# Feed-forward stage of a gated attention kernel: normalised x turned by HBM regrouping and VectorE instead of by TensorE

## What is computed

```
x = x + tanh(g_xattn) * attention(layernorm(x), ctx)      # 16 heads, 77 context rows
x = x + tanh(g_ffn)   * ffn(layernorm(x))

def ffn(x):
    hidden = x @ W1 + b1                                  # 512 -> 2048
    imag = w_imag * sin(theta + hidden * 0.1)
    phase = cos(theta) * w_real + sin(theta) * w_imag
    act = relu(hidden + phase * imag * 0.1)
    return act @ W2 + b2                                  # 2048 -> 512
```

## Time and profile before

| what | value |
|---|---|
| runs (three) | 2257.52, 2258.82, 2259.79 us |
| median | 2258.82 us |
| span of the profiled execution | 2257.7 us |
| TensorE busy | 2212.9 us, 98% |
| VectorE busy | 1412.5 us, 63% |
| ScalarE busy | 1210.5 us, 54% |
| GpSimd busy | 407.9 us, 18% |
| mean rate of the DMA | 61 GB/s |

### The profile page before, as it was taken

The page is one execution under the profiler, slowest core; times in us unless marked ns, Lnnn a source line. Parts: engine busy times, 40 slices in busy tenths (PEclk is TensorE's granted clock), DMA queues, the critical chain, the costliest instruction groups (busy, mean ns, idle before and its releaser), DMA issues.

```text
span 2257.7 us, 33637 instructions
## 1 busy us (share of the span) xinstructions
PE 2212.9 (98%) x10625; PEld 1850.6 (82%) x10625; DVE 1412.5 (63%) x2536; ACT 1210.5 (54%) x3571; POOL 407.9 (18%) x341
## 2 busy tenths in 40 slices
PE   8989999999999989999999999999999999999999
PEld 6778888888888877888888888888888888888887
DVE  5566776676677648656656556566565565665654
ACT  3477777776777746444444444444444444444443
POOL 5133333333333311101101011011011010110110
PEclk9999999999999999999999999999999999999999
DMA  7513222322322232101101101101011011011010
GB/s 228 178 33 99 80 84 77 103 80 79 93 86 81 83 134 86 55 19 38 56 19 37 56 19 37 56 0 56 19 37 56 19 37 56 19 37 53 3 38 19
DMA packets 136690, 137.92 MB, mean 61 GB/s; under 512 B 66128, under 2 KB 80988, under 8 KB 136586
## 3 DMA queue, kind: packets, MB, share of 16 engines
q1 hardware_dynamic: 134810, 136.16, 18.8%
q0 software_dynamic: 1344, 0.64, 0.2%
q10 hardware_dynamic: 432, 0.04, 0.0%
HBM read 93.13 MB, written 43.65 MB: 61 GB/s over the span
## 4 chain that ended last, share of the span: by engine, by line
PE 62%; DVE 1%; ACT 1%; issue 0%; ACTq 0%
PE m_bank L56 30%; PE pair_bank L56 30%; PE t_bank L1230 1%; DVE w_split L1332 0%; DVE hidden L1359 0%; ACT relu L1292 0%; DVE turns L1355 0%; ACT hidden L1301 0%; ACT turns L1303 0%; DVE stats L170 0%; DVE relu L1342 0%; DVE sine L1352 0%; ACT L1308 0%; ACT sine L1308 0%; ACT w_split L1288 0%
## 5 line engine op out<-in xcount | busy, mean ns | idle before, releaser
L56 PE MATMUL m_bank<-xT,w_split 128*128 128x512 f32 x3072 | 743.6, 391 | 4.0 <-DVE w_split L1332 4.0
L56 PE MATMUL pair_bank<-w_split,relu 128*128 128x512 f32 x3072 | 738.5, 389 | 2.0 <-DVE relu L1342 1.9
L56 PEld LDWEIGHTS pair_bank<-w_split,relu 128*128 128x128 f32 x3072 | 576.1, 188 | 123.6 <-issue 2.3
L56 PEld LDWEIGHTS m_bank<-xT,w_split 128*128 128x128 f32 x3072 | 576.3, 188 | 123.1 <-DVE w_split L1332 4.4
L1308 ACT ACTIVATE sine<-turns 128x512 f32<-128x512 f32 x256 | 161.8, 632 | 383.6 <-DVE turns L1355 383.6
L1292 ACT ACTIVATE relu<-hidden 128x512 fp32r<-128x512 f32 x256 | 161.9, 632 | 371.3 <-PE m_bank L56 286.2
L995 ACT ACTIVATE exps<-pair_bank,exp_bias 128x77 f32<-128x77 f32 x1024 | 318.7, 365 | 70.0 <-DVE exp_bias L1041 69.8
L1342 DVE SCALAR_TENSOR_TENSOR relu<-hidden,relu 128x512 fp32r<-128x512 f32 x256 | 180.9, 707 | 265.8 <-ACT relu L1292 265.8
L1359 DVE SCALAR_TENSOR_TENSOR hidden<-sine,sine_gain,hidden 128x512 f32<-128x512 f32 x256 | 197.1, 770 | 170.0 <-ACT sine L1308 170.0
L190 POOL TENSOR_TENSOR rstd<-var_eps,minus_half 128x4 f32<-128x4 f32 x32 | 38.2, 1195 | 1220.0 <-DVE var_eps L186 1220.0
L995 ACT ACTIVATION_READ_ACCUMULATOR exps<-pair_bank,exp_bias 128x1 f32 x1024 | 252.9, 247 | 0.0
(11 more groups left out here) (118 smaller groups left out, 1953.6 us busy)
## 6 DMA issues: line engine op xcount, KB each, us to landing
x_in<-in_x_dram SPq DMA_DIRECT2D x16, 1024.0 KB, 5.3
residual<-in_x_dram SPq DMA_DIRECT2D x64, 256.0 KB, 2.6
x_scratch<-residual SPq DMA_DIRECT2D x64, 256.0 KB, 2.0
x_in<-x_scratch SPq DMA_DIRECT2D x16, 1024.0 KB, 5.6
residual<-x_scratch SPq DMA_DIRECT2D x64, 256.0 KB, 3.3
out_dram<-residual SPq DMA_DIRECT2D x64, 256.0 KB, 2.1
w_chunk<-in_L_ffn_W_dram SPq DMA_DIRECT2D x16, 512.0 KB, 3.6
k_scratch<-kT SPq DMA_DIRECT2D x16, 308.0 KB, 4.7
```

Of the source, the lines that this page charges most:

```text
L56: mm = pe.matmul(out, stationary(s), moving(m), start=first and n == 0, stop=last and n == len(PASSES) - 1)
```

## The change

The 16 transposes of a batch on TensorE go. In their place:

1. SyncE waits until all four tiles of x are normalised and stores `x_in` to a new tensor in HBM, `quads`, in four DMAs, one for each c of 0 to 3 (`regroup_x`). DMA c takes from each partition the 16 runs of 32 numbers whose place in their 128 is c.
2. SyncE waits for all four stores and loads them back into `x_in`. DMA c fills the 32 partitions from 32c, each with four pieces of 512 numbers (2 KB).
3. VectorE turns each 32 x 32 block of `x_in` in place, with one `transpose` for each quarter a (128 partitions, 512 numbers): two behind step 9 and two behind step 10 (`TURN_AT`).
4. `x_hi` and `x_lo`, at steps 11 and 12 as before, read `x_in` through a pattern of runs of 32 numbers instead of `t_bank`.
5. The statistics move from behind step 3 to behind step 2, and normalisation from behind step 6 to behind step 4.
6. The next `load_x` waits for the lo parts (`t_split`) instead of the transposes (`t_full`).
7. In batch 0 the regrouping stands in SyncE's queue ahead of the load of chunk 10.

```diff
@@ -90,6 +90,8 @@
     NT = N // P
     FT = F // P
     G = D // P
+    BLOCK = 32
+    QUADS = P // BLOCK
     HG = P // DH
     GC = HG * M
     PC = -(-2 * GC // P)
@@ -112,6 +114,7 @@
     x1 = nc.dram_tensor("x1_scratch", [B, N, D], F32).ap()
     k_parts = nc.dram_tensor("k_scratch", [B, G, P, 2, M], F32).ap()
     v_parts = nc.dram_tensor("v_scratch", [B * M, 2, D], F32).ap()
+    quads = nc.dram_tensor("quad_scratch", [QUADS, P, NT * KT, BLOCK], F32).ap()
 
     ctx_rows = ctx_in.rearrange("b m d -> (b m) d")
     x_tiles = x.rearrange("b (t p) d -> b p t d", p=P)
@@ -1104,7 +1107,8 @@
 
         def ffn(st):
             AHEAD = 2
-            LN_AT, NORM_AT = 3, 6
+            LN_AT, NORM_AT = 2, 4
+            TURN_AT = {9: (0, 1), 10: (2, 3)}
             XT_AT = {9: (0, 1), 10: (2, 3)}
             w1_split = [sb(st, f"w1_split{i}", [P, KT, F], F32R) for i in range(2)]
             w2_split = [sb(st, f"w2_split{i}", [P, FT, D], F32R) for i in range(2)]
@@ -1118,7 +1122,9 @@
             b2_gated = sem(st, "b2_gated")
             chunk_hi = sem(st, "chunk_hi")
             chunk_split = sem(st, "chunk_split")
-            t_full = sem(st, "t_full_f")
+            quads_stored = [sem(st, f"quads_stored{c}") for c in range(QUADS)]
+            quads_loaded = sem(st, "quads_loaded")
+            blocks_turned = sem(st, "blocks_turned")
             t_hi = sem(st, "t_hi_f")
             t_split = sem(st, "t_split_f")
             h_full = sem(st, "h_full")
@@ -1138,6 +1144,11 @@
             residual_ready = sem(st, "residual_ready1")
             y_stored = [sem(st, f"y_stored1_{t}") for t in range(NT)]
 
+            x_quads = x_in[:, :, :].rearrange("p a (t k j) -> p t a k j", t=NT, k=KT)
+
+            def quad_order(tile):
+                return tile.rearrange("p (t a j) -> p t a j", t=NT, a=QUADS)
+
             block = st.enter_context(nc.Block())
 
             def over_batches(eng, batch):
@@ -1170,9 +1181,19 @@
                     sp.dma_start(residual[tile][:, :], x1_tiles[b, :, tile]).then_inc(residual_loaded[tile], 16)
 
                 def load_x(b):
-
-                    sp.wait_ge(t_full, KT * (b - 1))
+                    sp.wait_ge(t_split, KT * (b - 1))
                     sp.dma_start(x_in[:, :, :], x1_tiles[b]).then_inc(x_loaded, 16)
+
+                def regroup_x(b):
+                    sp.wait_ge(normed, NT * (B + b + 1))
+                    for c in range(QUADS):
+                        sp.dma_start(quads[c], x_in[:, :, :].rearrange("p t (k c j) -> p (t k) c j", c=QUADS, j=BLOCK)[:, :, c, :])\
+                          .then_inc(quads_stored[c], 16)
+                    for c in range(QUADS):
+                        sp.wait_ge(quads_stored[c], 16 * b)
+                    for c in range(QUADS):
+                        sp.dma_start(x_in[c * BLOCK:(c + 1) * BLOCK, :, :],
+                                     quads[c].rearrange("(a i) n j -> i a (n j)", i=BLOCK)).then_inc(quads_loaded, 16)
 
                 def store_y(b, tile):
                     sp.wait_ge(y_ready, NT * (b + 1) + tile + 1)
@@ -1191,11 +1212,17 @@
                     sp.wait_ge(x1_stored[tile], 16 * B)
                     load_residual(0, tile)
                 for n in range(STAGED, CHUNKS):
+                    if n == NORM_AT + 2 * STAGED:
+                        regroup_x(1)
                     sp.wait_ge(chunk_split, n - STAGED + 1)
                     load_chunk(sp, n)
-                with sp.Fori(0, B - 2) as b:
+                load_x(2)
+                outputs(0, False)
+                with sp.Fori(1, B - 2) as b:
+                    regroup_x(b + 1)
                     load_x(b + 2)
                     outputs(b, False)
+                regroup_x(B - 1)
                 outputs(B - 2, False)
                 outputs(B - 1, True)
                 for tile in range(NT):
@@ -1219,18 +1246,6 @@
 
             @block.tensor
             def _(pe):
-                def transpose_x(b, kts):
-
-                    pe.wait_ge(normed, NT * (B + b + 1))
-                    for kt in kts:
-                        if not (isinstance(b, int) and b == 1 and kt < 2):
-
-                            pe.wait_ge(t_split, KT * (b - 1) + kt - 1)
-                        for tile in range(NT):
-                            tr = pe.transpose(t_bank[kt % 2][:, tile * P:(tile + 1) * P],
-                                              x_in[:, tile, kt * P:(kt + 1) * P], ident[:, :])
-                        tr.then_inc(t_full, 1)
-
                 def first_product(b, slot, f):
                     if isinstance(b, int) and b == 0:
                         if f % HT == 0:
@@ -1268,8 +1283,6 @@
                         elif not last:
                             first_product(b + 1, 1 - slot, ahead - FT)
                         second_product(b, f)
-                        if f in XT_AT and not last:
-                            transpose_x(b + 1, XT_AT[f])
 
                 for f in range(AHEAD):
                     first_product(0, 0, f)
@@ -1279,8 +1292,9 @@
             def _(act):
                 def x_hi(b, slot, kts):
                     for kt in kts:
-                        act.wait_ge(t_full, KT * (b - 1) + kt + 1)
-                        act.activation(xT[slot][0][:, kt, :], t_bank[kt % 2][:, :], ACT.Copy).then_inc(t_hi, 1)
+                        act.wait_ge(blocks_turned, QUADS * b)
+                        act.activation(quad_order(xT[slot][0][:, kt, :]), x_quads[:, :, :, kt, :], ACT.Copy)\
+                           .then_inc(t_hi, 1)
 
                 def weight_hi(n):
                     raw, hi, _ = chunk_parts(n)
@@ -1331,11 +1345,17 @@
                     dve.wait_ge(chunk_hi, n + 1)
                     dve.tensor_tensor(lo, raw, hi.bitcast(F32), ALU.subtract).then_inc(chunk_split, 1)
 
+                def x_turn(b, groups):
+                    dve.wait_ge(quads_loaded, 16 * QUADS * b)
+                    for a in groups:
+                        dve.transpose(x_in[:, a, :], x_in[:, a, :]).then_inc(blocks_turned, 1)
+
                 def x_lo(b, slot, kts):
                     for kt in kts:
                         dve.wait_ge(t_hi, KT * (b - 1) + kt + 1)
-                        dve.tensor_tensor(xT[slot][1][:, kt, :], t_bank[kt % 2][:, :],
-                                          xT[slot][0][:, kt, :].bitcast(F32), ALU.subtract).then_inc(t_split, 1)
+                        dve.tensor_tensor(quad_order(xT[slot][1][:, kt, :]), x_quads[:, :, :, kt, :],
+                                          quad_order(xT[slot][0][:, kt, :].bitcast(F32)), ALU.subtract)\
+                           .then_inc(t_split, 1)
 
                 def relu_lo(b, f):
                     dve.wait_ge(relu_hi, FT * b + f + 1)
@@ -1377,6 +1397,8 @@
                                 statistics(dve, B + b + 2)
                             if f == NORM_AT:
                                 normalise(dve, B + b + 2)
+                            if f in TURN_AT:
+                                x_turn(b + 1, TURN_AT[f])
                             if f - AHEAD in XT_AT:
                                 x_lo(b + 1, 1 - slot, XT_AT[f - AHEAD])
                     if last:
```

## The result

| | before | after |
|---|---|---|
| median of the runs | 2259.31 us (4 runs, 2257.52 to 2260.37) | 2231.52 us (4 runs, 2227.58 to 2231.87) |
| span of the profiled execution | 2257.7 us | 2229.6 us |
| ratio, 95% interval | | 0.9876 (0.9863 to 0.9889) |

The change makes the kernel 1.2% faster, by 28 us (25 to 31 us by the interval). The forecast was 2233.8 us in a range of 2229 to 2256.

A forecast was written before the change was run, and what follows sets the result against it. The prediction took TensorE to set the pace in the feed-forward stage. Span 2257.7 - 27.0 for the transposes + 2.0 for batch 0 = 2232.7 us; with the median 1.1 us above the span, 2233.8 us, range 2229 to 2256.

The forecast's parts named there:

- Gain of TensorE: Feed-forward on TensorE: eight transposes cost 0.90 us, 16 a batch 1.8 us, so 15 batches gain 27.0 us.
- VectorE, steps 2 to 4: Earlier statistics and normalisation fit before second product 4 by 0.3 us; cost 0, bound 0 to 1 us a batch.
- The rival: VectorE has no room at step 4: TensorE waits 1 us in each of 15 batches, 2249 us; chance 0.12.
- The trip: Storing x to HBM and loading it back: 17.4 us a batch, inside the 26.0 us available.
- the keys' 84 ns: Upper case for a stored run, from the store of keys: stores 43 us, trip 54 us, kernel about 2650 us.
- The latest start: VectorE's first turn, wanted at 1417.5 when step 9 ends, must start by 1421.5 to be ready for second product 9.
- The rule of the Trainium skill: Stores below 512 B as read-modify-write: 25.2 ns a run, stores 12.9 us, trip 23.8 us, still inside.
- run 25: Not a follow-up run: a stored 128 B piece in the trip, put at 25.2 ns if moved twice.
- The turns: VectorE's 32 x 32 turns of 128 x 512: 0.75 us each; at 1.5 us each they would still cost nothing.
- Batch 0: Once, in batch 0: chunk 10 behind the stores 1 us, earlier statistics about 1 us, together 2 us.
- The sum: Whole kernel: 2257.7 - 27.0 + 2.0 = 2232.7 us of span, forecast median 2233.8 us.
- The rival on the slower side: Small stored runs late before step 9's turn: above 29 ns a run TensorE waits; at 40 ns 2315 us; chance 0.13.

The follow-up runs named there:

- e1: Changed kernel with 16 transposes a batch put back on TensorE at their old places, their result unread; 2258.46 us.
- e2: Kernel before the change with its feed-forward transposes left out and nothing in their place (output not the reference's); 2230.69 us.
- e6: Changed kernel with eight small memsets of unused PSUM added on VectorE behind the normalisation; 2245.87 us.
- e5: Changed kernel with statistics and normalisation moved back behind steps 3 and 6; 2232.29 us.
- e3: Changed kernel with the turns behind steps 6 and 7 instead of 9 and 10; 2361.93 us.
- e4: Changed kernel with the turns behind steps 7 and 8 instead of 9 and 10; 2238.27 us.
- e11: Changed kernel with turns behind steps 6 and 7 and stores in runs of 2 KB instead of 128 B (output not the reference's); 2250.47 us.
- e7: Changed kernel with the four stores done twice, to another tensor first; 2240.34 us.
- e10: Changed kernel with the trip's four loads filling 128 partitions with 2 KB each instead of 32 with four pieces (output not the reference's); 2232.27 us, single run.

## Why the prediction was right

**Gain of TensorE.** 0.90 us for eight transposes, 27.0 us in all: right. e1 gives 26.9 us for putting them back, and e2's floor is 28.6 us under the kernel before, with some 3 us of scatter in either.

**VectorE, steps 2 to 4.** Predicted slack before second product 4: 0.3 us; in the profile 0.53. The 9.7 us for the two steps beside GpSimd's rows were right: from 1372.1 to 1381.8. e6 shows that the slack is real and small. The rival's loss would have begun with relu_lo 0.53 us later, and its 1 us a batch needed 1.5 us.

**The trip.** 17.4 us predicted, 15.5 to 16.2 measured. Term by term: the stores' data 6.5 us at 12.6 ns a run, against 14.3 ns a run measured (7.3 us); with issue and landing 9.3 us, against 9.0; the way back 8.1 us, against the 6.5 to 7.2 us of e5. That last term was too large by 0.9 to 1.6 us. Three issues of up to 0.82 us were added to it, and they took 0.44 us each and ran beside the data. This hid a slower copy: the loads into 32 partitions take 154 ns for 2 KB, against 0.89 x 16 x 2048 B / 316 GB/s = 92 ns in the earlier trace rows. That a stored run would cost about what a loaded one does was in no row. It came out, though nothing in the trace before could tell; at the keys' 84 ns the change would have lost.

**The latest start** was put 4.0 us behind the wanted one at step 9. No run made the trip that late there: e5's waits, 2.9 us and at most 3.5, reach no one. But the same reckoning holds at two other steps. At step 6 it leaves 1395.66 - (1390.53 + 0.75) - 1.30 - 0.69 = 2.4 us, at step 7 1401.10 - (1395.04 + 0.75) - 1.99 = 3.3 us. In e3 8.3 us of VectorE's wait reach TensorE with 5.7, or 2.6 us less; in e4 3.6 us reach it with 0.45, or 3.2 us less.

**The rule of the Trainium skill** (DMA: Bandwidth & Descriptors, Specifications) that under 512 B a transfer is done as read-modify-write would have made a run 25 ns. The stores' 14.3 ns show no such doubling of the loaded run for runs of 128 B that are stored side by side. Whether a smaller price of that kind is in the 14.3 ns no run shows, and scattered runs were not tried.

**The turns** take 687 ns and not 750. x_hi and x_lo, whose durations the prediction kept, went from 584 to 616 ns and from 683 to 684 ns. **Batch 0** was put at 2 us and measured 1.5 (52.94 against 51.45). Chunk 10 cost 0.3 us of it, since ScalarE waited 3.2 us and all but that was slack.

**The sum.** Feed-forward begins in the two profiles, before and after, with

```profile
828.07 11.07 PE L56 MATMUL m_bank<-xT,w_split 128*128 128x512 f32 x36 [3.95 <-DVE w_split L1332]
...
825.78 10.93 PE L56 MATMUL m_bank<-xT,w_split 128*128 128x512 f32 x36 [3.96 <-DVE w_split L1346]
```

and from there to the end it takes 2257.7 - 828.1 = 1429.6 us against 2229.6 - 825.8 = 1403.8. That is 25.8 us less, where the prediction had 27.0 - 2.0 = 25.0 and, with the 1.5 us measured for batch 0, 25.5 were to come. The other 2.3 us of the spans' 28.1 lie in the stages before, whose code is the same; 13 runs of the kernel before, beside these experiments, lie between 2253.2 and 2261.8 us, so this is within the scatter. So is the distance of the median from the forecast, 2.3 us.

**The rival on the slower side** (the small runs are late) did not come, since it needed 29 ns a run. But its mechanism is right, as e3 shows: VectorE's wait, relu_lo behind it, second product behind that. Its price was counted as the lateness alone, 5.4 us late for +81 us. e3 was 5.7 late and cost 130, since the clock falls behind such a wait. Had the runs cost 40 ns, an estimate by e3 is 15 x (5.4 + 2.6) = 120 us more than the forecast, near 2354 us and not 2315.

## What to carry to other kernels

Where TensorE sets the pace and its groups follow one another without a gap, an instruction taken off it gives back its pitch, and any longer way round is free if it ends before the latest start of its reader; so work out that latest start from the timeline and compare it with the trip, rather than asking whether the trip is long. Keep some distance from it: TensorE's waits of 3.1, 5.9 and 7.5 us (e11, e3, e7) were dearer than their length by some 2.5 us each. Look for the tightest place beside it (here 0.53 us behind the moved normalisation) and for what stands behind the new waits in a shared queue (here one weight chunk in batch 0). And don't move what need not move: in e5 the early normalisation, the riskiest part of the change, buys nothing that the medians can tell.

## What the runs showed that was not expected

- A wait of TensorE of 5.9 us is followed by a group at half clock (granted 0.50, 1.2 GHz): 5.29 us to the next start instead of 2.72. Waits of 3.1 us (e11, batch 0) and 7.5 us (e7, batch 0) are followed by the same, 5.26 and 5.16 us. After waits of 0.5 to 1.4 us (e6, e11) the clock stays at 1.00 and the next group is 0.1 to 0.2 us longer.
- A load into 32 partitions, four pieces of 2 KB in each, takes 154 ns of an engine for 2 KB, and into 128 partitions 103 ns (e10). The trip would end 1 us sooner by it.
- A store of 2048 runs holds SyncE's queue for 1.24 us (median of 60; 0.44 us with 2 KB runs), so SyncE could issue nothing else for 5.5 us while the four stores went out.
- Runs of 128 B stored to HBM take 14.3 ns each, against 12.6 ns for loaded ones.
